# Four attention layers and four expert layers in one kernel: the last router fed with raw rows and ranks summed by TensorE, and the last three attention tiles in another order

## What is computed

```python
Q = rope((q @ Wq))            # 16 heads of 64, K and V of 4 groups
attn = softmax(Q K^T * scale + rel_pos_bias)
x = x + (attn V) @ Wo
# last layer, E = 8 experts, C = 320 places each
xf = layernorm(x)
eid = argmax(softmax(xf @ router_w + router_b))
rank = cumsum(onehot(eid))[token] - 1        # earlier tokens of the same expert
valid = rank < C
y = relu(buf[eid, rank] @ w1[eid] + b1) @ w2[eid] + b2   # if valid
y = relu(xf @ ow1 + ob1) @ ow2 + ob2                     # overflow, if not
```

## Time and profile before

| | us |
|---|---|
| median of 3 runs | 1017.33 |
| the three runs | 1013.89, 1018.5, 1017.33 |
| the profiled execution | 1013.49 |
| its span, first to last instruction | 1011.7 |
| PE busy in it | 902.6 (89%) |
| DVE, ACT, POOL busy | 676.6, 421.3, 376.5 |
| mean granted clock of TensorE | 0.968 of full speed |

### The profile page before, as it was taken

One profiled execution on the slowest core, in us unless ns is written; L12 is line 12 of the kernel. 1 busy time (PEld: TensorE's weight loads), 2 busy tenths in 40 slices (PEclk: granted clock), 3 DMA queues, 4 the chain that ended last, 5 costly groups with the idle time before them and its releaser, 6 DMA issues. The chain is left out here.

```text
span 1011.7 us, 17450 instructions
## 1 busy us (share of the span) xinstructions
PE 902.6 (89%) x5825; PEld 642.4 (63%) x5832; DVE 676.6 (67%) x1619; ACT 421.3 (42%) x1133; POOL 376.5 (37%) x279
## 2 busy tenths in 40 slices
PE   2899989999889985868899889999999839999997
PEld 2687744444478864743487547777777517778786
DVE  5899967987689988876377687878768631222221
ACT  2466640000155656753355345556664403122222
POOL 1676402433467722516455313333333410110111
PEclk9999999999999997988899999999999969999999
DMA  6100079999700008102366382311111148534200
GB/s 208 59 1 0 1 205 251 312 306 285 247 1 1 0 1 222 52 16 95 113 188 202 117 262 72 113 51 51 51 51 36 44 143 299 203 98 152 93 12 20
DMA packets 87260, 117.18 MB, mean 116 GB/s; under 512 B 12464, under 2 KB 75949, under 8 KB 86781
## 3 DMA queue, kind: packets, MB, share of 16 engines
q1 hardware_dynamic: 77455, 88.15, 29.4%
q10 hardware_dynamic: 4408, 15.46, 4.6%
q0 software_dynamic: 5328, 12.70, 3.5%
HBM read 68.08 MB, written 50.16 MB: 117 GB/s over the span
## 5 line engine op out<-in xcount | busy, mean ns | idle before, releaser
L1016 PE MATMUL psum<-m_W,lnT 128*128 128x512 f32 x256 | 114.2, 598 | 0.6 <-DVE acc L928 0.6
L410 POOL TENSOR_TENSOR prob<-prob,a_rden 128x1232 f32<-128x1232 f32 x30 | 67.5, 2250 | 58.1 <-DVE a_rden L506 58.1
L1016 PEld LDWEIGHTS psum<-m_W,lnT 128*128 128x128 f32 x256 | 47.2, 190 | 59.0 <-issue 55.8
L2907 ACT ACTIVATE prob<-psum,x_b 128x320 f32<-128x320 f32 x64 | 33.8, 527 | 120.8 <-PE psum L2964 120.8
L2575 PE MATMUL psum<-g_VW,pT 128*128 128x256 f32 (+1 forms) x320 | 72.5, 382 | 1.6 <-ACT pT L2465 1.5
L1001 POOL TENSOR_TENSOR m_masked<-m_rel,m_mrow 128x1232 f32<-128x1232 f32 x16 | 42.2, 2647 | 84.5 <-DMA masked_bias<-m_masked 62.2
L2765 POOL DMA_INDIRECT out_x<-x_yt,x_X x20 | 19.8, 992 | 137.3 <-DVE x_yt L2846 137.3
L2575 PEld LDWEIGHTS psum<-g_VW,pT 128*128 128x128 f32 (+1 forms) x320 | 59.5, 190 | 11.2 <-issue 3.7
L2234 POOL TENSOR_TENSOR g_qr<-g_t 128x1024 f32<-128x1024 f32 x15 | 35.5, 2364 | 74.1 <-DVE g_t L2307 74.1
L2527 PE MATMUL psum<-g_Wq,lnT 128*128 128x512 f32 x128 | 59.1, 605 | 1.0 <-ACT lnT L2439 1.0
L2241 POOL TENSOR_TENSOR prob<-prob,g_rden 128x1232 f32<-128x1232 f32 x15 | 33.7, 2248 | 68.3 <-DVE g_rden L2342 68.3
(11 more groups left out here) (472 smaller groups left out, 2240.7 us busy)
## 6 DMA issues: line engine op xcount, KB each, us to landing
routed_rows<-hole SPq DMA_DIRECT2D x8, 2210.0 KB, 36.8
masked_bias<-m_masked ACTq DMA_DIRECT2D x16, 616.0 KB, 8.2
g_bias<-masked_bias SPq DMA_DIRECT2D x16, 616.0 KB, 3.9
m_xb<-routed_rows SPq DMA_DIRECT2D x39, 130.0 KB, 2.0
m_rel<-in_rel_bias ACTq DMA_DIRECT2D x8, 616.0 KB, 10.9
expert_rows<-hole SPq DMA_DIRECT2D x1, 4680.0 KB, 36.7
g_early_w<-in_L_ffn_w SPq DMA_DIRECT2D x8, 512.0 KB, 4.7
g_early_w<-in_L_ffn_w SPq DMA_DIRECT2D x4, 1024.0 KB, 5.7
```

The lines of the kernel that those rows point to most:

```text
L410: nc.gpsimd.tensor_tensor(heads(c.prob[b]), heads(c.prob[b]), rden[b][:, :].unsqueeze(2).to_broadcast([P, H, SK]), ALU.mult).then_inc(norm ...
L1016: last = nt.matmul(c.ps[p][:, :], c.lnT[b][:, k * P:(k + 1) * P], W[:, k, p * 512:(p + 1) * 512], start=(k == 0), stop=(k == KC - 1))
```

## The change

In the router:
- The rows are transposed as they are, not normalised. `router_w` loses the mean of its column once, in step 0 (column sums by PE with a matrix of ones, subtraction by DVE), which takes off the row's mean; the logits are multiplied by `rstd` in `first_expert`. The twelve instructions of L2358 and the four of L2794 go. `router_w` is loaded second on SP's list, `router_b` and the triangle matrix behind one more load.
- The one-hot is written as bf16 straight away, the cast goes.
- PE sums the ranks. All matmuls go into one region of a bank: one with the triangle for the tile itself, and for each distance `shift` one with ones, which adds the one-hots of the tiles that far back to the group's columns. `pe_earlier_ranks` does those that need only earlier groups (11 for group 1, 16 for group 2) ahead of the wait for the group's own one-hot, `pe_ranks` the rest (8, 4 and 5 matmuls in the three groups). The last group has one column block more, the total.
- `slots` has eight instructions instead of sixteen; `first_slot` (one instruction, three in later groups) goes.
- In `moe3` PE's ten fillers and its wait for `ln_ok` go; ACT copies the transposes ahead of the square root; a square root on a spare tile at the end of ACT's list in `attn_gqa` loads the table ahead of the barrier; `row_statistics` comes behind `first_expert`.
- The scatters of tiles 8 to 11 move from `moe3` to the end of POOL's list in `attn_gqa`.

In the last three tiles:
- PE, step 14: behind the probability transposes of tile 13 come the query transposes of tile 15, the router's transposes and the scores of tile 15, and only then `output(13)`. The ten fillers go. Step 15 has no scores.
- DVE: rope(15), shift(14), route(14), shift(15), sums(14), finished(13), sums(15), route(15), finished(14), places(15), finished(15), where `finished` is the residual sum and the statistics.
- ACT: `qT_copy(15)` ahead of `exps(14)`; `exps(15)` first in step 15.
- `mx` and `den` get a second buffer.

```diff
@@ first_expert
+                     c.rstd[:, ones8].rearrange("p (g t) -> p g t", t=2).unsqueeze(3).to_broadcast([P, n // 2, 2, 8]),
+                     ALU.mult).then_inc(read, 1)
     dve.wait_ge(read, nth)
+    chain(nv.tensor_tensor(tiles(lg), tiles(lg), r.rb.unsqueeze(1).to_broadcast([P, n, 8]), ALU.add))
...
-    chain(nv.tensor_tensor(tiles(hot), tiles(tmp), wide(first), ALU.is_equal))
-    return nv.tensor_copy(r.ohb[:, eights], hot)
+    return nv.tensor_tensor(tiles(hot), tiles(tmp), wide(first), ALU.is_equal)
@@ slots
+    nv.tensor_scalar(over8, ranks[:, 0:n * 8], -float(CAP), 0.0, ALU.add, ALU.max)
+    nv.tensor_tensor(rank8, ranks[:, 0:n * 8], r.ohb[:, eights], ALU.mult).then_inc(read, 1)
     dve.wait_ge(read, nth)
...
+    nv.reduce_sum(over, tiles(over8), AX)
     chain(nv.reduce_sum(rank, tiles(rank8), AX))
...
+    chain(nv.scalar_tensor_tensor(out=slotf, in0=c.first[:, ones8], scalar=-float(CAP), in1=rank, op0=ALU.mult, op1=ALU.add))
+    chain(nv.tensor_tensor(slotf, slotf, over, ALU.subtract))
+    chain(nv.scalar_tensor_tensor(out=slotf, in0=rank, scalar=float(CAP), in1=slotf, op0=ALU.is_lt, op1=ALU.mult))
+    return nv.scalar_tensor_tensor(out=r.slot[:, ones8], in0=slotf, scalar=float(E3 * CAP), in1=over, op0=ALU.add, op1=ALU.add)
@@ ranks
+def rank_tiles(u):
+    lo, n = ROUTED[u]
+    return lo, n, n + (lo + n == NT)
+
+def pe_count(c, r, u, bank, shift, first, last, start=False):
+    lo = ROUTED[u][0]
+    return c.nc.tensor.matmul(bank[:, (first - lo) * 8:(last - lo) * 8], r.onesb, r.ohb[:, (first - shift) * 8:(last - shift) * 8],
+                              start=start, stop=True, skip_group_check=True)
+
+def pe_earlier_ranks(c, r, u, bank):
+    lo, n, wide = rank_tiles(u)
+    shifts = [*range(wide, lo + 1), *range(1, wide), *range(lo + 1, lo + wide)]
+    for shift in shifts:
+        pe_count(c, r, u, bank, shift, max(lo, shift), min(lo + wide, lo + shift), start=shift == shifts[0])
@@ attn_gqa, DVE
-        for t in range(-1, NT + 1):
+        for t in range(-1, NT - 2):
             step(t, t % 4)
+        rope(NT - 1, (NT - 1) % 2)
+        shift(NT - 2, (NT - 2) % 4)
+        route(NT - 2)
+        shift(NT - 1, (NT - 1) % 4)
+        sums(NT - 2, NT % 2)
+        finished(NT - 3)
+        sums(NT - 1, (NT - 1) % 2)
+        route(NT - 1)
+        finished(NT - 2)
+        places(NT - 1)
+        finished(NT - 1)
@@ attn_gqa, PE
-                wait(pe, s["pT_ok"], i * 3 - 5 + u)
+                wait(pe, s["pT_ok"], i * 3 - 3 if i == NT - 1 and u == 0 else i * 3 - 5 + u)
...
+            if t == NT - 2:
+                q_transpose(NT - 1, 1 - b)
+                route(t)
+                scores(NT - 1, 1 - b)
             if inside(t - 1):
                 output(t - 1, 1 - b)
...
-            if t == NT - 2:
-                keep_warm(c, c.ps[0], 10)
@@ attn_gqa, POOL
+        pool.wait_ge(s["r_slot_ok"], 2)
+        for k in range(HALF, ROUTED[2][0]):
+            scatter_tile(c, r, k)
@@ moe3
-            for k in range(LAST, NT):
-                nv.tensor_scalar(c.lnk[:, k * D:(k + 1) * D], xt(c, TOKEN_ORDER[k]), mean_of(c, k), rstd_of(c, k),
-                                 ALU.subtract, ALU.mult).then_inc(s["ln_ok"], 1)
...
-            keep_warm(c, c.ps[3], 10)
...
+            pe_earlier_ranks(c, rt, 2, bank_rank)
             pe.wait_ge(s["oh_ok"], 1)
```

More of the change, by code:

```diff
@@ L1118, in __init__ @@
         self.ohb = c.lg2[:, 0:NT * 4].bitcast(BF16)
[L1119 to L1120 removed]
         m = HALF * 8
[L1122 removed]
         self.rank8, self.over8 = c.acc[1][:, 0:m], c.acc[1][:, m:2 * m]
[L1124 removed]
+        self.rank, self.over, self.slotf = (c.acc[1][:, 2 * m + u * HALF:2 * m + (u + 1) * HALF] for u in range(3))
         self.slot = c.acc[1][:, 2 * m + 4 * HALF:2 * m + 4 * HALF + NT].bitcast(U32)
@@ L2356, in route @@
                 chain(nv.reciprocal(c.rstd[:, ones8], c.std[:, ones8]))
-                for k in range(ones8.start, ones8.stop):
-                    nv.tensor_scalar(c.lnk[:, k * D:(k + 1) * D], xt(c, tile(k)), mean_of(c, k), rstd_of(c, k),
-                                     ALU.subtract, ALU.mult).then_inc(s["r_ln_ok"], 1)
+            if t == 0:
+                dve.wait_ge(s["r_sum_ps"], 1)
+                for k in range(KC):
+                    nv.scalar_tensor_tensor(out=r.rw[:, k, :], in0=bank_y[:, 0:RW], scalar=-1.0 / D, in1=r.rw[:, k, :],
+                                            op0=ALU.mult, op1=ALU.add).then_inc(s["r_rw_ok"], 1)
             if t == HALF + 2:
@@ L2384, in places, with finished @@
             if t == HALF + 7:
-                first_slot(c, r, 1, chain)
                 dve.wait_ge(s["r_pre_ps"], 2)
                 slots(c, dve, r, 1, c.ps[0], chain, s["r_pre_read"], 2).then_inc(s["r_slot_ok"], 1)
+        def finished(i):
+            residual(i, i % 2)
+            dve.wait_ge(s["x_ok"], i + 1)
+            nv.tensor_copy(c.gap[:, i % 2:i % 2 + 1], c.ones[:, 0:1])
+            stats = nv.bn_stats(bst_of(c, i), xt(c, tile(i)))
+            if i + 1 in (HALF, HALF + 4):
+                chain(stats)
         def step(t, q):
@@ L2402, in step @@
             if inside(t - 1):
-                residual(t - 1, 1 - b)
-                dve.wait_ge(s["x_ok"], t)
-            if inside(t - 1):
-                nv.tensor_copy(c.gap[:, b:b + 1], c.ones[:, 0:1])
-                stats = nv.bn_stats(bst_of(c, t - 1), xt(c, tile(t - 1)))
-                if t in (HALF, HALF + 4):
-                    chain(stats)
+                finished(t - 1)
             if t % 4 == 0 and inside(t + 7):
@@ L2615, in step @@
             banks_read(t)
-            if inside(t):
+            if inside(t) and t < NT - 1:
                 scores(t, b)
+            if t == 0:
+                pe.wait_ge(s["r_w_in"], 16)
+                for k in range(KC):
+                    last = nt.matmul(bank_y[:, 0:RW], c.ones[:, :], r.rw[:, k, :], start=(k == 0), stop=(k == KC - 1))
+                last.then_inc(s["r_sum_ps"], 1)
             if t == HALF + 7:
@@ L2756, in _ @@
             ng = nc.gpsimd
-            for k in range(HALF, LAST):
-                scatter_tile(c, rt, k)
             pool.wait_ge(s["slot_ok"], 1)
```

109 lines of the change are left out of this document (43 added, 66 removed).

## The result

The changed kernel takes 1019.28 us (median of 20 runs, 1014.72 to 1028.46), the kernel before 1016.31 beside it (20 runs, 1012.18 to 1024.44): ratio 1.004, 95% interval [1.0024, 1.0056]. It is slower, by 3.0 us between the medians and by 4 us as the ratio has it; the forecast was 2.4 us faster, and 1019.28 lies above its range.

A forecast was written before the change was run, and what follows sets the result against it. The prediction took an unforked chain of waits, from the barrier at 805 us through the last router to the expert matmuls, as the bound. Terms -4.2 +1.2 +0.6 gave -2.4 us, 1014.9 on the median; range 1010.5 less 0.5, to 1018.5.

The forecast's parts named there:

- The step that failed: Ahead of the barrier: POOL's four early scatters end at 803.4, hidden beneath TensorE's end, so the barrier is 1.2 us later.
- Rival 4: At the barrier: POOL's four scatters end behind TensorE and the barrier waits for them, perhaps for landing; +1.2 us, chance 0.08.
- the router: Last router, behind the barrier: slots done 8.3 us behind the release for 12.5, saving 4.2 us.
- TensorE's end: Last tiles of the grouped attention: TensorE's last filler ends at 804.6 for 803.4, so the barrier is 1.2 us later.
- The clock's term of +0.6: Last router without fillers: TensorE's clock may fall to 1.2 GHz, costing 1.2 us; half was put in.
- The counts: Rank matmuls on TensorE at 0.065 us each: sixteen take 1.04 us, hidden in a 1.5 us stretch; eleven take 0.72.
- The new order: Last three tiles: the 3.1 us stall turns into waits of 1.2 and 2.1 us, and the barrier comes 1.2 us later.
- wait of 1.04: Grouped attention: TensorE waits 1.04 us for ScalarE's copy before scoring tile 15, part of 3.1 us another order could win.
- rival 2: Last tiles: TensorE's clock falls behind the 2.1 us wait for tile 14, costing 1.7 us; 1016.6 us, chance 0.17.
- The earlier edits: Ahead of the last tiles: column sums, dropped LN instructions and moved small loads change nothing; uncovered column sums, half a microsecond.
- The second fall of the clock: Expert matmuls, 831.6 to 835.0: 3.4 us at half speed lose 1.7 us, kept both ways, so 0.
- Rival 3: Last tiles: the serial string from rope(15) to POOL's product comes 1.3 us late and the clock falls; 1018.5, chance 0.08.

The follow-up runs named there:

- experiment 1: The changed kernel with the grouped attention's block closed without GpSimd's drain, scatters still early: 1007.86 us, ratio 0.9968 to the kernel before.
- experiment 2: The changed kernel with the scatters of tiles 8 to 11 put back behind the barrier, drain kept: 1009.21 us, ratio 0.9977; run again later, 0.9962.
- experiment 3: The kernel before with only the four scatters of tiles 8 to 11 moved ahead of the barrier: 1023.49 us, ratio 1.0131.
- experiment 4: The changed kernel with one of the four scatters ahead of the barrier and three behind it: 1020.05 us, beside 1017.64 for the kernel before.
- experiment 8: experiment 2 with eight filler matmuls in TensorE's wait for tile 14's product: 1004.71 us, ratio 0.9919; run again side by side, 0.9945.
- experiment 9: Three kernels: experiment 5 without its ten fillers, 0.9902; the changed kernel with old tile order and no drain, 0.993; both together, 0.991.
- experiment 5: experiment 2 with the last three tiles in the old order and its ten fillers: 1004.09 us, ratio 0.9933; again 0.9924 and 0.9956.
- experiment 6: experiment 2 with VectorE's sums(14) ahead of shift(15) and ScalarE's wait set to match: 1015.08 us, ratio 0.998.

## Why the prediction was wrong

**The step that failed** is the last of the tail: four scatters "end at 803.4, beneath TensorE's end by 1.2. They were hidden before too", and from it "the barrier is 1.2 us later". The scatters were timed right: with scores(13) as zero they were to end at 44.1, and they ended at 44.2. What fell was the assumption that the barrier asks for the end of the scatter. It asks for the drain behind it, which ends 6.84 us later, and the barrier came 6.9 us later than before instead of 1.2 (experiments 1 to 4). Rival 4 named this place, and priced it with the landing, 2.4 us behind the issue: +1.2, chance 0.08. With the drain it is +6.1 on TensorE's end, which turns the sum's sign. It could have been read from the trace of before: the drain of 15.4 us at L144 ended 6.5 us behind the last scatter, with 2.9 to spare. Moved scatters were costed by their own durations alone, and the prediction never asked what the engine's last instruction ahead of the barrier was. Term by term, the router gave -4.0 where -4.2 and +0.6 were forecast, TensorE's end +0.8 where +1.2 was, the drain +6.1 where there was no term, and the stages behind the last scatter, put at nothing, +1.1.

**The router** was forecast at 8.3 behind the release and, with half a clock fall, at 8.9. In after, where the stall put the clock at 0.50, it is 8.51, 4.0 saved. Where the barrier doesn't stall and the clock is up it is 7.12 to 7.14 (experiments 1, 8 and 9 and the second trace of 2), 5.4 saved where 4.2 was forecast. The logits start 1.85 behind the release (1.98), logits to one-hot take 3.52 (4.13), one-hot to slots 1.75 (2.2). Of the 0.6 in the middle none is the cast: `first_expert` and the way to it take 1.99 from the transposed logits to the one-hot, for 1.90 in before. What went is a pause of that one execution: in the trace of before ScalarE's copy of the logits starts 0.74 behind the end of the logits' row, in experiment 1 0.05, and in experiment 3, which has the old router, 0.05 as well. So 4.13 was too long for either router by 0.7, and without the pause the saving is 4.7, nearer to the 4.2. In experiments 5 and 6 the slots came at 7.88 with the clock up: the rows of the rank matmuls end where they do elsewhere, 5.7 behind the release, but VectorE, which waits for them, starts at 6.49 instead of 5.74. This is the pause of before in another place, a signal of TensorE's that comes some 0.75 late; why, I can't say. The clock's term of +0.6, half of 1.2, was a fall in two of eleven undisturbed traces, at 0.6 and 1.0 us to the slots.

**The counts** cost next to nothing: sixteen in 0.56 us and eleven in 0.42, or 0.035 and 0.038 each, for 0.065 assumed; in the trace the sixteen start 0.026 us apart on average. The Trainium skill ("TensorE: Matmul & The Clock Gate", section "Wait — 56ns, not 53.3ns?") says that the starts of small matmuls never come closer together than about 25 ns, and has about 62 ns for each only where hardware decoding is off; the rows here agree with the first figure.

**The new order** was walked rightly: waits of 1.34 and 1.92 for 1.2 and 2.1, TensorE's end 0.8 later for 1.2. But it was set against the wrong thing. With the router edits the old order gets rid of its wait of 1.04 by itself, and stands at 42.88, or 41.74 without fillers; so the order costs 2.0 to 3.1 us against what could be had, and its wait brings rival 2's fall of the clock, 1.7 as priced, in half of the traces for the chance of 0.17. The Trainium skill ("TensorE: Matmul & The Clock Gate", section "Why this matters for your kernels") advises against idle stretches between bursts of matmuls. The traces agree for the 7.7 us at the barrier of after, with a clock of 0.50 behind them; for the wait of 1.92 they show a tendency, a fall in three of six, and none in the two where it was filled.

**The earlier edits** at nothing: 165.6 us from scores(0) to scores(13) in both kernels, as forecast. The second fall of the clock, at the expert matmuls, is in every readable trace but one, at varying length, and no edit moved it in a way that I can tell from chance. From the first expert matmul to the end it is 179.8 to 181.5 us in those, and 178.6 in the one without it, the second trace of experiment 2, where the clock is 1.00 for the first 10 us of the expert matmuls. So the 1.7 us that the prediction had for this fall is about right (1.5 between that trace and before's).

**Rival 3**, the late string, did not come: the long instruction of the first slots is there (L1159, 0.88 us), and the wait it would have lengthened is 1.92.

**What stays open.** The tail's clock: why it falls behind the same wait of 1.92 in one execution and not in the next. Why the tail of GpSimd's drain goes with the block's indirect DMAs. And whether the new order costs 0.1% or 0.4% in time over many executions: the same pair of kernels came out 0.44% apart in one session and 0.06% in another, with the traces at 0.2 and the clock's share on top.

## What to carry to other kernels

Give an early issue its place by the event that it gates, not by its duration; here four scatters gated nothing early, since the last group's slots came last either way. And when two edits are made together, cost each against the kernel with the other one in: the router edits had removed by themselves the wait for which the order was changed.

## What the hardware showed unexpectedly

- GpSimd's drain at the end of a block ends 6.52, 6.60 and 6.84 us behind the end of the last of 79, 80 and 83 indirect DMAs in the block, and 2.51 to 2.71 behind the last of 28 to 32. Where the landing can be read, the first of these came 4.8 to 5.0 us after the last one had landed, and the third 5.2. In blocks without an indirect DMA the drain ends within 0.1 us of GpSimd's last instruction.
- After 7.7 us without any work TensorE's clock was at 0.50 in the transposes and 0.56 in the logits (1.94 and 1.82 us, against 1.32 and 1.06 us in experiment 1).
- A run of sixteen matmuls of 8 to 40 columns each takes 0.56 us; they start 0.026 us apart.
- The time of one kernel moves by some 10 us between executions (before in one session: 1005.6 to 1016.9). In the traces the largest part of it lies ahead of the grouped attention: from the first barrier to scores(0) it was 208.5 to 224.9 us, where the kernels differ by three small loads alone.
